# An adaLN block with attention and 32 experts on one core: expert outputs are added into three planes in memory instead of stored into six

## What is computed

```python
x = x + ga * attention(h)
h = layernorm(x) * (1 + cb) + sb
shared_out = silu(h @ shared_gate_w.T) * (h @ shared_up_w.T) @ shared_down_w.T
routing_weights = softmax(h @ router_weight.T)          # 32 experts
_, top_idx = top_k(routing_weights + e_score_bias, 6)   # 6 experts of each token
combine[token, top_idx] = routing_weights / their sum
hmid = silu(gate) * up                                  # per expert, 128 wide
y = einsum('tei,ehi->teh', hmid, down_proj)
out = einsum('teh,te->th', y, combine) + shared_out     # sum over 6 experts
x = x + gb * out
```

## Time and profile before

| | |
|---|---|
| median of 3 runs | 802.63 us (802.34 to 802.96) |
| profiled execution: span, first to last instruction | 799.6 us |
| what lies around the span, against the median of the runs | 3.0 us |
| PE busy | 740.7 us, 93% of the span |
| DVE, ACT, POOL busy | 480.8, 400.0, 411.3 us |
| mean granted TensorE clock | 0.972 |
| DRAM read, written | 88.15 MB, 73.57 MB |

### The profile page before, as it was taken

One profiled execution on the slowest core, in us unless ns is written; L12 is line 12 of the kernel. 1 busy time (PEld: TensorE's weight loads), 2 busy tenths in 40 slices (PEclk: granted clock), 3 DMA queues, 4 the chain that ended last, 5 costly groups with the idle time before them and its releaser, 6 DMA issues.

```text
span 799.6 us, 13266 instructions
## 1 busy us (share of the span) xinstructions
PE 740.7 (93%) x4302; PEld 590.7 (74%) x4302; DVE 480.8 (60%) x1207; ACT 400.0 (50%) x943; POOL 411.3 (51%) x420
## 2 busy tenths in 40 slices
PE   4989999999999898969999899999999999999963
PEld 4465667657657555549999799999999999997521
DVE  3676678879869954533555244444544544446986
ACT  5267574874464174115655455555565655662000
POOL 0000000267777777777777766765666666666000
PEclk9996999999999999989999999999999999999997
DMA  9420001024235896556676866765765666677995
GB/s 327 132 80 1 0 1 54 34 107 177 116 123 218 315 393 235 227 196 230 227 255 218 284 219 216 230 220 165 226 202 179 194 204 199 194 265 265 363 413 222
DMA packets 82605, 158.45 MB, mean 198 GB/s; under 512 B 14430, under 2 KB 55523, under 8 KB 82280
## 3 DMA queue, kind: packets, MB, share of 16 engines
q1 hardware_dynamic: 58344, 96.74, 36.9%
q0 software_dynamic: 19968, 56.67, 17.8%
q10 hardware_dynamic: 4224, 4.19, 1.5%
HBM read 88.15 MB, written 73.57 MB: 202 GB/s over the span
## 4 chain that ended last, share of the span: by engine, by line
PE 69%; DVE 9%; POOL 8%; DMA 5%; issue 4%; ACT 3%; SPq 2%; DVEq 0%; ACTq 0%; POOLq 0%
PE ps_wide L1320 17%; PE ps_wide L1335 12%; PE ps_kv L1320 8%; PE ps_wide L1089 8%; POOL expert_rows L541 8%; PE ps_narrow L1308 6%; DMA arena<-expert_outs 2%; PE ps_wide L1082 2%; PE ps_wide L1111 2%; PE ps_kv L1344 2%; PE ps_narrow L1040 1%; PE ps_narrow L1102 1%; PE ps_kv L1111 1%; DMA arena<-expert_rows 1%; DMA arena<-w_g 1%
## 5 line engine op out<-in xcount | busy, mean ns | idle before, releaser
L541 POOL DMA_INDIRECT expert_rows<-arena,slot_i x192 | 193.3, 1007 | 215.7 <-DVE arena L1638 151.2
L647 POOL DMA_INDIRECT expert_outs<-arena,meta x224 | 217.8, 972 | 111.7 <-DVE arena L1842 69.6
L894 ACT COPY arena<-arena 128x512 f32 x224 | 127.4, 616 | 157.0 <-PE ps_narrow L1308 153.4
L1842 DVE TENSOR_SCALAR arena<-ps_wide,meta 128x256 f32<-128x256 f32 x224 | 98.1, 479 | 129.9 <-PE ps_wide L1335 129.4
L1320 PEld LDWEIGHTS ps_wide<-arena 128*128 128x128 f32 x1200 | 148.4, 195 | 4.0 <-issue 0.2
L1320 PE MATMUL ps_wide<-arena 128*128 128x128 f32 x1200 | 149.0, 278 | 0.0
L1335 PE MATMUL ps_wide<-arena 128*128 x448 | 116.1, 382 | 0.9 <-DVE arena L1818 0.5
L1335 PEld LDWEIGHTS ps_wide<-arena 128*128 128x128 f32 x448 | 76.8, 191 | 7.4 <-issue 1.5
L1089 PE MATMUL ps_wide<-arena 128*128 128x512 f32 x168 | 75.4, 597 | 2.8 <-DVE arena L1532 2.8
L1308 PE MATMUL ps_narrow<-cst,arena 128*128 128x128 f32 x448 | 69.2, 277 | 7.9 <-DMA arena<-expert_rows 7.8
L1320 PEld LDWEIGHTS ps_kv<-arena 128*128 128x128 f32 x592 | 71.8, 192 | 1.9
(11 more groups left out here) (235 smaller groups left out, 1012.3 us busy)
## 6 DMA issues: line engine op xcount, KB each, us to landing
arena<-expert_rows SPq DMA_DIRECT2D x224, 160.0 KB, 2.8
arena<-expert_outs SPq DMA_DIRECT2D x48, 512.0 KB, 13.2
arena<-w_experts SPq DMA_DIRECT2D x32, 384.0 KB, 8.3
expert_rows<-pad_row SPq DMA_DIRECT2D x33, 160.0 KB, 5.0
out<-x ACTq DMA_DIRECT2D x8, 512.0 KB, 10.1
expert_outs<-arena,meta POOLq DMA_INDIRECT x224, 3.1
x<-x SPq DMA_DIRECT2D x3, 1024.0 KB, 11.1
h_cols<-arena SPq DMA_DIRECT2D x6, 512.0 KB, 3.8
```

The lines of the kernel that those rows point to most:

```text
L541: nc.gpsimd.indirect_dma_start(rows, bass.IndirectOffsetOnAxis(ap=slots_i[b % 2][:, t, k:k + 1], axis=0), hrows[b % 2][:, t, :], None, bou ...
L647: nc.gpsimd.indirect_dma_start(outs, bass.IndirectOffsetOnAxis(ap=meta_i[:, j % METAS, 1:2], axis=0), yb[j % OUTS], None, bounds_check=las ...
L894: last = nc.scalar.copy(wgu[:, j % 4:j % 4 + 1, :], wall[:, bass.ds(expert[j], 1), 0:DOWN])
L1842: v.tensor_scalar(yb[j % OUTS], ps_wide[:, 1, p % 2, j % DUO * D:(j % DUO + 1) * D], meta[:, j % METAS, 0:1], None, ALU.mult).then_inc(s_y ...
```

## The change

The stores of the expert blocks become accumulating DMAs (`compute_op=ALU.add`): block j is added to plane j mod 3, at the row of its token. The three planes (4096 token rows and 128 rows for padding each) are filled with zeros from `pad_row` by three DMAs on SP's queue early in the program, and POOL waits for them (`s_zero`) once. Since two blocks of different experts may hold the same token, POOL waits before store j until store j - 3, the last one into the same plane, has landed. Every row's number is now just its token; the scan that counted a token's choices goes from `rows_of_slots` (DVE). Padding rows are added to the planes' last 128 rows, so they are written now.

The tail loads three planes to a part, into a set of buffers for each of the 8 parts; 7 parts may be loaded once the real blocks are stored, the last part after the last block. PE sums two of the three planes of a part and DVE's `close` adds the third; in parts 5 and 7 PE sums all three (and `close` has one pass less), in part 0 it takes one and DVE adds the other two.

Part 5 of the shared expert is done with parts 0 to 4, ahead of the blocks; none is left in the tail. Its input is loaded behind the last expert weights.

```diff
-FIN = 4
-BY_PE = [[3, 4, 5] if n in (3, 5, 7) else [4, 5] for n in range(8)]
-BY_DVE = [[k for k in range(TOPK) if k not in by_pe] for by_pe in BY_PE]
+PLANES = 3
+PLANE_ROWS = T + P
+BY_DVE = [[0, 1] if n == 0 else [] if n in (5, 7) else [0] for n in range(8)]
+BY_PE = [[k for k in range(PLANES) if k not in by_dve] for by_dve in BY_DVE]
...
-BEFORE = 5
-LAST, AMONG = [BEFORE], [BEFORE + 1, BEFORE + 2]
-TAIL = [0, 1, 2, LAST[0], 3, 4] + AMONG
+BEFORE = 6
+AMONG = [BEFORE, BEFORE + 1]
+TAIL = list(range(BEFORE)) + AMONG
...
-CLEAR = FIN - 1
+CLEAR = PARTS - 1
...
+            for q in range(PLANES):
+                sp.dma_start(outs[q].rearrange("(n p) d -> p n d", p=P),
+                             pad_row[:, None, 0:D].to_broadcast([P, PLANE_ROWS // P, D])).then_inc(s_zero, 16)
...
+            sp.wait_ge(s_slot, B + 1)
+            load_h2(BEFORE - 1)
...
             def load_planes(n):
 
-                if n >= FIN:
-                    sp.wait_ge(s_res, n - FIN + 1)
                 first = ORDER[TAIL[n]] * PART * P
-                for k in BY_PE[n] + BY_DVE[n]:
-                    sp.dma_start(fin[n % FIN][k], outs[k * T + first:k * T + first + PART * P, :].rearrange(
-                        "(p t) d -> p t d", p=P)).then_inc(s_fin_pe[n] if k in BY_PE[n] else s_fin[n], 16)
+                for k in range(PLANES):
+                    sp.dma_start(fin[n][k], outs[k][first:first + PART * P, :].rearrange(
+                        "(p t) d -> p t d", p=P)).then_inc(s_fin[n], 16)
 
             for u in range(UNROLL):
                 sp.wait_ge(s_put[u], written[u])
             for n in range(CLEAR):
                 load_planes(n)
-            for u in range(UNROLL):
-                sp.wait_ge(s_put[u], 16 * ROUNDS // LAPS)
             sp.wait_ge(s_y, DUOS)
             for n in range(CLEAR, PARTS):
                 load_planes(n)
+            for u in range(UNROLL):
+                sp.wait_ge(s_put[u], 16 * ROUNDS // LAPS)
...
+            pool.wait_ge(s_zero, 16 * PLANES)
             for j in range(BLOCKS):
                 u = j % UNROLL
+                if j >= PLANES:
+                    old = j - PLANES
+                    pool.wait_ge(s_put[old % UNROLL], (old // UNROLL + 1) * 16)
                 pool.wait_ge(s_yc, j + 1)
-                nc.gpsimd.indirect_dma_start(outs, bass.IndirectOffsetOnAxis(ap=meta_i[:, j % METAS, 1:2], axis=0),
-                                             yb[j % OUTS], None, bounds_check=last_out,
-                                             oob_is_err=False).then_inc(s_put[u], 16)
+                nc.gpsimd.indirect_dma_start(outs[j % PLANES], bass.IndirectOffsetOnAxis(ap=meta_i[:, j % METAS, 1:2], axis=0),
+                                             yb[j % OUTS], None, bounds_check=last_out, oob_is_err=True,
+                                             compute_op=ALU.add).then_inc(s_put[u], 16)
...
             for i in range(2, BEFORE):
+                if i == BEFORE - 1:
+                    act.wait_ge(s_sd, BEFORE - 1)
                 shared_silu(i)
...
-            pe.wait_ge(s_yc, BLOCKS)
-            shared_gate_up(LAST[0])
             for n in range(1, PARTS):
                 sum_planes(n)
```

More of the change, by code:

```diff
@@ L96, in adaln_block_kernel @@
         h2_cols = nc.dram_tensor("h2_cols", (PARTS - 2, P, C, HALF), F32, kind="Internal").ap()
-        outs = nc.dram_tensor("expert_outs", (OUT_ROWS, D), F32, kind="Internal").ap()
+        outs = [nc.dram_tensor(f"expert_outs{q}", (PLANE_ROWS, D), F32, kind="Internal").ap() for q in range(PLANES)]
         gate_rows = nc.dram_tensor("gate_rows", (1, B, 2, D), F32, kind="Internal").ap()
@@ L154, in adaln_block_kernel @@
         at[0] = 0
-        fin = [[take(PART, D) for _ in range(TOPK)] for _ in range(FIN)]
-        assert at[0] <= wall_end and CLEAR * PART * TOPK * D <= (E - 1) * WCOLS
+        fin = [[take(PART, D) for _ in range(PLANES)] for _ in range(PARTS)]
+        assert at[0] <= wall_end and CLEAR * PART * PLANES * D <= (E - 1) * WCOLS
         at[0] = 0
@@ L226, in adaln_block_kernel @@
         counted_at = at[0]
-        mask, planes, not_first = (take(TILES, E) for _ in range(3))
+        mask = take(TILES, E)
+        take(2 * TILES, E)
         slot8 = take(TILES, 8)
@@ L268, in adaln_block_kernel @@
         mid = ([late[0], late[2]] + [take(C, HALF, overlay=h2_at + i * C * HALF) for i in range(2)]
[L269 removed]
+               + [tail_in[1], tail_in[1]])
         rope_rows = take(2, TILES, HW, overlay=rope_at)
@@ L338, in adaln_block_kernel @@
         s_fin = [sem(f"s_outputs_in{i}") for i in range(PARTS)]
-        s_fin_pe = [sem(f"s_outputs_in_for_tensor{i}") for i in range(PARTS)]
+        s_zero = sem("s_planes_zeroed")
         s_acc, s_read, s_res = sem("s_planes_summed"), sem("s_planes_read"), sem("s_result")
@@ L995, in shared_down @@
                 last.then_inc(s_sd, 1)
[L997 to L1004, removed]
             def count(late_half, ps):
@@ L1408, in sum_planes @@
                     pe.wait_ge(s_read, n - 1)
-                shares = TAIL[n] in LAST
-                pe.wait_ge(s_fin_pe[n], 16 * len(BY_PE[n]))
+                pe.wait_ge(s_fin[n], 16 * PLANES)
                 for a in range(2):
                     for k in BY_PE[n]:
[L1413 to L1416, removed]
+                        last = mm(summed[n % 2][:, a], ident, fin[n][k][:, 2 * a:2 * a + 2, :],
+                                  start=(k == BY_PE[n][0]), stop=(k == BY_PE[n][-1]))
                 last.then_inc(s_acc, 1)
-            def shared_gate_up(i):
-                shared_gate(i)
-                shared_up(i)
             pe.wait_ge(s_xbc, DUOS)
@@ L1632, in rows_of_slots @@
                     v.tensor_tensor(pairs[:, :, :, 0], comb, psm[:, :, None].to_broadcast(wide), ALU.mult)
[L1634 to L1637 removed]
+                    link(v.tensor_scalar(pairs.bitcast(U32)[:, :, :, 1], tok[:, :, None].to_broadcast(wide), 0.0, None, ALU.add))
                     v.tensor_scalar(tok, tok, float(S), None, ALU.add).then_inc(s_slot, 1)
@@ L1892, in close @@
             def close(n):
-                f = fin[n % FIN]
+                f = fin[n]
                 part = x2[:, ORDER[TAIL[n]] * PART:(ORDER[TAIL[n]] + 1) * PART, :]
+                by_pe = summed[n % 2][:].rearrange("p a (t d) -> p (a t) d", d=D)
                 dve.wait_ge(s_acc, n + 1)
-                v.tensor_tensor(f[0], f[0], summed[n % 2][:].rearrange("p a (t d) -> p (a t) d", d=D), ALU.add).then_inc(s_read, 1)
-                dve.wait_ge(s_read, n + 1)
-                link(v.tensor_tensor(f[0], f[0], gate_of(ORDER[TAIL[n]]), ALU.mult))
-                v.tensor_tensor(part, part, f[0], ALU.add).then_inc(s_res, 1)
-            add_planes(0)
-            close(0)
-            add_planes(1)
-            shared_mid(LAST[0])
-            close(1)
-            for n in range(2, PARTS):
+                if BY_DVE[n]:
+                    v.tensor_tensor(f[0], f[0], by_pe, ALU.add).then_inc(s_read, 1)
+                    dve.wait_ge(s_read, n + 1)
+                    link(v.tensor_tensor(f[0], f[0], gate_of(ORDER[TAIL[n]]), ALU.mult))
+                else:
+                    v.tensor_tensor(f[0], by_pe, gate_of(ORDER[TAIL[n]]), ALU.mult).then_inc(s_read, 1)
+                    dve.wait_ge(s_read, n + 1)
+                v.tensor_tensor(part, part, f[0], ALU.add).then_inc(s_res, 1)
+            for n in range(PARTS):
                 add_planes(n)
```

26 lines of the change are left out of this document (10 added, 16 removed).

## The result

The changed kernel takes **865.9 us** (median of 4 runs), the kernel before 802.8 us beside it: 1.077 times as long, 95% interval 1.074 to 1.079. I had forecast 772.5 us, in a range of 768 to 836. The profiled execution has a span of 861.2 us. One of the four runs took 995 us and is not in the ratio.

A forecast was written before the change was run, and what follows sets the result against it. The prediction took the blocks to be bound by PE, their start by row scatters and the tail by the planes' bytes: 799.6 - 31.1 + 1.0 = 769.5 us of span, plus 3.0 around it 772.5 us, range 768 to 836.

The forecast's parts named there:

- Then POOL's wait is over before DVE delivers, and it costs 0: Expert blocks' stores: an adding store lands in 4.1 us, so waiting for store j - 3 adds no time.
- The sum: Whole kernel: 799.6 - 31.1 + 1.0 = 769.5 us of span, 772.5 us with the 3.0 us around it.
- the case beside it: Rival on POOL: issuing an adding store takes 1.46 us for 0.97, 48 us more, 820 us; chance 0.10.
- the formula: POOL's time in the store stage, 224 x 1.76 + 32 x 1.27 = 435 us with dearer issue, for what has 387.
- the two rivals: POOL's stores: the wait for store j - 3 sets the pace (834 us, chance 0.16); issuing gets dearer (820 us, 0.10).
- The landing: Adding stores in the blocks: 4.1 us from start of issue to landing, between 3.1 and 5.9 us.
- The slack: Blocks: 14 output buffers let POOL be about 11 blocks, 17 us, behind PE before stores begin to cost.
- The DMA engines: DMA share in the blocks: 0.75 to 0.95 where it was 0.72, still under a full queue's 1.04.
- The tail: 24 loads in place of 48, none waited for, PE's sums 29.2 us: 31.1 us less.
- The head: Start of the blocks: part 5 of the shared expert done ahead costs 1 us more, bounds 0 and 10.3.

The follow-up runs named there:

- e8: The changed kernel with half of each row (512 bytes in place of 1024) added, zeroed and read back: 847.0 us, 1.053 of the kernel before.
- e1: The changed kernel with plain stores in place of adding ones, all else kept: 775.2 us, 0.965 of the kernel before.
- Six chains: The changed kernel with adding stores into six zeroed planes in turn, store j waiting for j-6, the tail reading three: 859.5 us, 1.068 of the kernel before.
- e10: The changed kernel with plain stores and four small waited-for memsets on POOL behind each store: 922.2 us, 1.147 of the kernel before.
- e5: The kernel before with only the zeroing added, three DMAs into planes nobody reads: 806.3 us against 805.3.
- e6: The kernel before with SP's wait for the last stores moved behind the tail's last loads: 800.7 us against 805.3, 0.9931.
- e7b: The kernel before with SP's last wait behind the loads and PE summing three planes of every part, part 5 in the tail: 803.0 us, 0.9966.
- e4: The kernel before with only part 5 of the shared expert moved ahead of the expert blocks: 807.4 us against 805.3, 1.0030.
- e7: The kernel before with SP's last wait behind the loads, PE summing three planes of every part, and part 5 ahead of the blocks: 801.6 us, 0.9947.
- e2: The changed kernel with padding rows numbered past the planes' end, so the store's bounds check skips them: 858.2 us, 1.069 of the kernel before.

## Why the prediction was wrong

- *"Then POOL's wait is over before DVE delivers, and it costs 0"* is the step that failed. The sum had an issue of 0.97 us in it, and the only row for it was that of a plain store. The text priced the case beside it (1.46 us, 820 us, a chance of 0.10) and argued against it that scatters and stores cost the same whatever they carry; that was true of the bytes, as e8 shows, and says nothing of the kind of DMA. With the measured 1.54 us the formula gives 224 x 1.84 + 41 = 453, 66 over 387, and 838 us. The remaining 28 us have the size by which the stage is longer than 453: the two rivals came together, the wait for landings on top of the dearer issue, and I had added up each alone. Part of that equality is chance. The chain leaves POOL at store 209. That one goes out 442.7 us after the first, where 209 x 1.84 + 32 x 1.27 gives 425: 17 us of waits. It then lands 7.35 us after its start, beside the tail's loads, and only then can the last weighing go. What POOL waits for after it, 11 of its 33 us, is off the chain. From e1 to the change the last weighing moves from about 739 to 824.6, 86 of the 88 us between the two spans.
- *The landing* was estimated at 4.1 us and measured at 4.7 (3.5 to 8.8). Without the issue it is 3.2 us for 2.1 before: the 1.0 us that I had added was right in size, the missing 0.6 are the issue again. Six chains show that this wait is worth some 6 us of the 91 with the tail as it is; with the tail's bytes halved as well (e8) 19 us went.
- *The slack*: I let POOL fall 17 us behind for nothing. That counted 14 buffers and left out that the last scatters stand behind store 95 on the same queue; PE's wait of 14.8 us shows it. Since POOL is busy all through that wait, it did not itself lengthen the stage.
- *The DMA engines*: forecast at 0.75 to 0.95, measured at 0.97. In e1 POOL's queue takes 19.6% of 773.5 us, 152 us; in the change 36.3% of 861.2, 313 us, for the same 60.84 MB. If the stores' part in e1 is that of their bytes (29.4 MB), 73 us, adding makes it 234, three times as much. The Trainium skill (Collectives: The Full Stack, "The bandwidth ceiling: the fold count and why AG ≠ RS ≠ AR") says half the rate, that is twice the time, and says it of the reducing step in a ring of cores; this trace, by the estimate by bytes above, does not agree for indirect stores. The load on the DMA engines did not bound the blocks, by e8 and e10.
- *The tail* was right: 29.3 us of PE without a wait for a load in e1, and from PE's first sum to the end of the span 35.1 us (738.38 to 773.5) in place of 66.4 (733.25 to 799.6): 31.2 us less for 31.1 forecast. That the time with plain stores came as near as 775.2 to 772.5 is in part luck: the span was 773.5 for 769.5, but 1.9 us lay around it and not 3.0. In the change itself it takes from 816 to 861, since its loads go out at 800.6, DVE waits for the last buffers, and one part of PE's work runs at the lower clock (6.60 us from 827.52, at a granted clock of 0.55, for what takes 3.43 us behind it, at 1.00).
- *The head* of the blocks: 1 us forecast. The fourth gate-and-up group starts at 367.67 us before, 368.45 in e5, 369.87 in e6 and 370.49 in e7b, which have part 5 in the tail. With part 5 ahead it starts at 372.65 in the change, 372.96 in e4, 373.14 in e7 and 371.48 in e1, and between 370.3 and 374.3 in the other variants of the changed kernel with three planes. These are single executions that differ by 3 to 4 us among themselves; the means, 369.1 and 372.5, put part 5 at some 3 us. Zeroing three planes costs nothing that could be measured.

## What to carry to other kernels

Halving the bytes of a bound stage is worth what the engine that has to do it can spare. Here the tail did lose 31 us, but POOL, which issues the stores, had 370 - 256 x 1.27 = 45 us to spare in the store stage, gaps counted, and was asked for 224 x 0.57 = 128 us more. Before an operation of a new kind goes into a loop, measure its time on the engine that issues it; the price of its plain relative is not a price. And where two new costs meet on one queue, price them together: issue, gap and wait for landing add up.

## What the runs showed of the hardware

- An adding indirect DMA of 128 rows keeps GpSimd for 1.54 us, a plain one for 0.97; with 64 rows 1.40, with rows half as wide 1.54, with rows skipped by the bounds 1.54. A plain one behind an adding one takes 1.03 us. Why the adding one costs more is not shown.
- Packets of POOL's queue for a store: 48 with plain stores, (41,472 - 192 x 48) / 224 = 144 with adding ones, 80 for adding ones of 64 rows, (27,136 - 9,216) / 224: one packet a row and 16 more. Rows that the bounds skip (e2) leave the packets at 41,472 and take only their bytes away, 56.68 MB for 60.84.
- A tiny memset with a wait for its own semaphore costs GpSimd about 0.24 us (0.95 us for four).
